# One recommendation tower, first stage: a DMA moved to another queue, one piece of work moved to ScalarE

## The reference

```python
e = stack([tbl_f[ids[:, f]] for f in range(27)], axis=1)      # 512 x 27 x 128
z = einsum('bnd,bmd->bnm', e, e)[:, i, j]                     # pairs i < j: 512 x 351
h = concatenate([z, dense_ctx], axis=1)                       # 512 x 367
h = maximum(h @ W_top1 + b_top1, 0)                           # 512
h = maximum(h @ W_top2 + b_top2, 0)                           # 256
y = h @ W_top3                                                # 512 x 1
```

## Time and profile before

| | us |
|---|---|
| median of 3 runs | 110.33 (110.22 to 110.46) |
| the profiled execution | 109.96 |
| its span in the profile | 107.8 |
| busy: PE, DVE, ACT, POOL | 99.6, 73.8, 70.4, 65.9 |

### The profile page before, as it was taken

One profiled execution on the slowest core, in us unless ns is written; L12 is line 12 of the kernel. 1 busy time (PEld: TensorE's weight loads), 2 busy tenths in 40 slices (PEclk: granted clock), 3 DMA queues, 4 the chain that ended last, 5 costly groups with the idle time before them and its releaser, 6 DMA issues.

```text
span 107.8 us, 2420 instructions
## 1 busy us (share of the span) xinstructions
PE 99.6 (92%) x993; PEld 84.2 (78%) x993; DVE 73.8 (68%) x68; ACT 70.4 (65%) x100; POOL 65.9 (61%) x71
## 2 busy tenths in 40 slices
PE   4995999999999799999999879999999999997992
PEld 4993887777767687876778679999998897996790
DVE  3299999999999999999999943035245405622131
ACT  5039999999999999999999956144404241421021
POOL 3177788777787777787777787777777720005000
PEclk9999999999999999999999999999999999999999
DMA  1899688888869694869526412679653443034100
GB/s 42 192 365 340 167 301 292 207 257 300 223 250 250 193 305 135 239 207 222 177 49 204 185 49 55 213 131 253 222 93 78 150 128 53 9 132 81 24 0 1
DMA packets 13031, 18.26 MB, mean 169 GB/s; under 512 B 7601, under 2 KB 8446, under 8 KB 13020
## 3 DMA queue, kind: packets, MB, share of 16 engines
q1 hardware_dynamic: 9552, 12.90, 39.8%
q0 software_dynamic: 2016, 4.06, 13.8%
q10 hardware_dynamic: 1452, 1.14, 3.5%
HBM read 16.32 MB, written 1.77 MB: 168 GB/s over the span
## 4 chain that ended last, share of the span: by engine, by line
PE 43%; DVE 37%; issue 9%; DMA 8%; ACT 1%; SPq 0%; ACTq 0%; DVEq 0%
DVE hot L474 25%; PE psG L359 13%; DVE parts L479 10%; PE psG L340 8%; PE psG L386 5%; PE psH L402 5%; PE psT L318 4%; DMA pick_ids<-in_picked_ids 4%; PE psH L340 3%; PE psH L371 3%; DMA pair_grams<-gram 3%; DMA zT<-pair_grams 2%; PE psH L417 1%; DVE hot L460 1%; DVE hot L463 1%
## 5 line engine op out<-in xcount | busy, mean ns | idle before, releaser
L301 POOL DMA_INDIRECT rows<-in_tbl,ids_sb x61 | 63.6, 1042 | 21.7 <-issue 18.3
L340 PE MATMUL psG<-hot,parts 128*128 128x512 f32 x196 | 49.5, 401 | 2.4 <-ACT hot L564 1.2
L340 PEld LDWEIGHTS psG<-hot,parts 128*128 128x128 f32 x196 | 35.2, 188 | 13.5 <-DVE hot L474 4.8
L474 DVE TENSOR_TENSOR hot<-pick_ids,psH 128x1536 fp32r<-128x1536 int32 (+2 forms) x23 | 41.5, 1843 | 0.0
L560 ACT ACTIVATE hot<-pick_ids,row_no 128x512 fp32r<-128x512 int32 (+1 forms) x30 | 19.4, 710 | 0.0
L479 DVE TENSOR_TENSOR parts<-table,parts 128x1024 fp32r<-128x1024 f32 (+1 forms) x12 | 16.2, 1349 | 0.0
L564 ACT ACTIVATE hot<-hot 128x1024 fp32r<-128x1024 f32 (+2 forms) x12 | 15.0, 1247 | 0.4
L359 PEld LDWEIGHTS psG<-ET 128*54 128x54 f32 x512 | 13.3, 130 | 2.3 <-issue 1.6
L359 PE MATMUL psG<-ET 128*54 128x54 f32 x512 | 13.9, 213 | 1.3 <-issue 1.2
L487 DVE COPY gram<-psG 128x432 f32<-128x432 f32 x8 | 7.3, 911 | 10.8 <-PE psG L359 10.8
L571 ACT COPY gram<-psG 128x432 f32<-128x432 f32 x8 | 7.3, 914 | 11.2 <-PE psG L359 10.5
(11 more groups left out here) (31 smaller groups left out, 49.7 us busy)
## 6 DMA issues: line engine op xcount, KB each, us to landing
table<-in_tbl SPq DMA_DIRECT2D x6, 640.0 KB, 4.8
table<-in_tbl SPq DMA_DIRECT2D x6, 512.0 KB, 5.5
pick_ids<-in_picked_ids SPq DMA_DIRECT2D x11, 256.0 KB, 4.0
rows<-in_tbl,ids_sb POOLq DMA_INDIRECT x61, 3.8
pair_grams<-gram SPq DMA_DIRECT2D x4, 216.0 KB, 2.3
pair_grams<-gram ACTq DMA_DIRECT2D x4, 216.0 KB, 3.0
w_sb<-in_w SPq DMA_DIRECT2D x1, 768.0 KB, 4.4
w_sb<-in_w SPq DMA_DIRECT2D x1, 512.0 KB, 4.3
```

Of the source, the lines that this page charges most:

```text
L301: pool.indirect_dma_start(out=rows[:, n % RING, x, :], out_offset=None, in_=gathered_tables[f], in_offset=bass.IndirectOffsetOnAxis(ap=ids ...
L340: last = pe.matmul(picked_psum(k), parts[:, k % 2, x, c, :], hot[:, k % 2, c, looked_up(k)], start=x == 0 and c == 0, stop=x == 1 and c == ...
L474: dve.tensor_tensor(hot[:, k % 2, first:end, looked_up(k)], pick_ids[:, k % TABLES, looked_up(k)].unsqueeze(1).to_broadcast(shape), number ...
```

## The change

The DMA of `ids_sb` goes from the head of SP's queue to ScalarE's queue, behind the one that ScalarE had. BY_ACT[0] becomes 3 instead of 2, so ScalarE makes three chunks of the first table's `hot` and VectorE five instead of six. Two of these three distances are computed ahead of `split_high(0)`, the third behind it.

```diff
-    BY_ACT = [2 if chunks == min(CH) else 3 for chunks in CH]
+    BY_ACT = [2 if chunks == min(CH) and k > 0 else 3 for k, chunks in enumerate(CH)]
...
         def _(sp):
-            sp.dma_start(ids_sb[:, :, :], ids).then_inc(ids_in, 16)
             for k in range(FP):
...
-            def make_last_hot(k):
-
+            def distances(k, chunks):
                 if k == 0:
                     act.wait_ge(first_ids_in, 16)
                 act.wait_ge(pick_ids_in[k], 16)
-                chunks = range(CH[k] - BY_ACT[k], CH[k])
                 for c in chunks:
                     act.activation(hot[:, k % 2, c, looked_up(k)], pick_ids[:, k % TABLES, looked_up(k)], ACT.Abs, bias=row_number(k, c),
                                    scale=-1.0).then_inc(distance_ready, 1)
+
+            def make_last_hot(k):
+                first = CH[k] - BY_ACT[k]
+                distances(k, range(first + 2 if k == 0 else first, CH[k]))
                 act.wait_ge(distance_ready, sum(BY_ACT[:k + 1]))
-                last = hot[:, k % 2, chunks[0]:CH[k], looked_up(k)]
+                last = hot[:, k % 2, first:CH[k], looked_up(k)]
                 act.activation(last, last, ACT.Relu, bias=1.0, scale=-1.0).then_inc(last_hot_ready, 1)
...
             act.dma_start(pick_ids[:, 0, 0:B // 2], picked_ids[0, 0:B // 2].partition_broadcast(V)).then_inc(first_ids_in, 16)
+            act.dma_start(ids_sb[:, :, :], ids).then_inc(ids_in, 16)
...
             act.wait_ge(row_no_ready, 2)
+            distances(0, range(CH[0] - BY_ACT[0], CH[0] - BY_ACT[0] + 2))
             split_high(0)
             make_last_hot(0)
```

## The result

The changed kernel takes 111.76 us as the median of four runs (111.27 to 112.93), the kernel before 110.28 in the same comparison (109.29 to 110.46): a ratio over the fast runs of 1.0186, with a 95% interval of 1.0131 to 1.0242. The two medians are 1.48 us apart, which is 1.3%, while the ratio says 1.9%: the change is slower, clear of noise, by 1.3 to 2.4%. I had forecast 110.6, within 109.7 to 111.1, so the measured time lies above the range. The profiled execution took 111.27 at a span of 109.4, against 109.96 at 107.8.

What follows compares the result with a forecast made beforehand. VectorE paced TensorE during the picks, ScalarE nearly level, GpSimd's gathers 0.85 us ahead of quad 15. TensorE's 0.55 gain is lost waiting for the delayed last gather: +0.23 on the 110.33 median gives 110.56, about 110.6 (109.7 to 111.1).

Steps and rivals of the forecast that it cites:

- hidden fourth chain: GpSimd's 61 gathers, absent from the chain of waits, run without gaps to quad 15, the last landing at 88.49.
- slack of 0.85 at quad 15: Before the change, the last gather lands at 88.49, only 0.85 us ahead of quad 15's weight loads at 89.34.
- the gain of the picks: At the handover from picks to first product, ScalarE's lead makes TensorE about 0.55 us earlier.
- the sign of being wrong: Last gather starting before 86.3 or after 88, or TensorE not stopping ahead of quad 15, would refute the prediction.
- The hold and the lost place: Gathers starting inside line 479's subtraction are held to its end; the third, not fourth, is held, losing one place.
- the landing of `ids_sb`: At the kernel's start, `ids_sb` lands between 4.6 and 5.6, taken as 5.0, 0.85 us later than now.
- rival C: At the first subtraction, the second gather is held, two places lost: another 1.25 us, 111.8; chance 0.16.
- VectorE's gain: At the first table, line 479 starts at 7.83 instead of 8.19, 0.36 us earlier, set by the table's landing.
- From the split to the next table's: ScalarE's work behind the first table's landing takes 3.15 us instead of 3.37, saving 0.22.
- transfers that hang on it: From handover to quad 15, TensorE's work and dependent transfers carry the 0.55 us gain through, reaching quad 15 at 88.8.

Runs made afterwards that it cites:

- e7: Changed kernel with line 478's second operand read from PSUM (low parts not the reference's): 109.44 us against 109.42 for the kernel before, ratio 1.0010.
- e9: Kernel before plus a GpSimd memset of 2500 columns between the landing of `ids_sb` and the first gather: 110.32 us against 109.35, ratio 1.0110.
- e10: Kernel before plus a GpSimd memset of 3200 columns between the landing of `ids_sb` and the first gather: 111.4 us against 109.35, ratio 1.0154.
- e11: Kernel before with `ids_sb` second on ScalarE's queue and the small b1 load in its place at SP's head: 110.06 us, ratio 1.0062.
- e1: Changed kernel with `ids_sb` back at the head of SP's queue: 149.9 us against 150.4 in a slow batch, times not used.
- e5: Changed kernel with `ids_sb` back at the head of SP's queue, on another chip: 109.48 us against 109.42 for the kernel before, ratio 1.0001.
- e8: Kernel before plus a GpSimd memset of 500 columns between the landing of `ids_sb` and the first gather: +0.4 us, ratio 1.0028.
- e2: Kernel before with only the DMA of `ids_sb` moved to ScalarE's queue: 153.0 us against 150.4 in a slow batch, times not used.
- e4: Changed kernel with `ids_sb` issued by GpSimd: 153.3 us against 150.4 for the kernel before in a slow batch, times not used.
- e6: Kernel before with only the DMA of `ids_sb` moved to ScalarE's queue, on another chip: 112.16 us against 109.42, ratio 1.0288.
- e3: Changed kernel with ScalarE's two queued DMAs exchanged, `ids_sb` first: 151.3 us against 150.4 for the kernel before in a slow batch, times not used.
- e12: Changed kernel with `ids_sb` at SP's head and the first table second on ScalarE's queue: 110.5 us, ratio 1.0122 to the kernel before.

## Why the prediction was wrong

*The bound and the hidden fourth chain: right.* The gathers' slack of 0.85 at quad 15 was the thing to watch; the gain of the picks (ScalarE's copy at 61.46, forecast 61.4; first product at 62.16, forecast 62.05) came to nothing, and TensorE stopped where I said, for 1.66 us instead of 0.7. The last gather started at 88.29, behind the 88 that I gave as the sign of being wrong.

*The hold and the lost place: right, and shown by e7, e9 and e10.* The Trainium skill, "SBUF — State Buffer", section "SBUF: two separate sides", lists two kinds of VectorE operation that take the pair of ports from GpSimd: one in a two-port mode, which I cited, and one with two SBUF inputs, the latter only against a GpSimd operation that reads SBUF. e7 points to the second: with one operand from PSUM the duration stays at 1.22 and every hold is gone. So does the kernel before: a gather that starts inside the comparison of line 474, which has one operand in SBUF and one in PSUM, isn't held (6.58 for 0.98, in the 1.75 us from 6.51 on).

*The step that failed: the landing of `ids_sb`, "1.17 + 3.4 = 4.6 at the earliest and 1.17 + 4.4 = 5.6 at the latest", of which I took 5.0.* It landed at 6.6. The upper bound was the wrong row: the 4.4 us of the second DMA on SP's queue was measured with nothing of SP's moved forward, and e11 gives 4.6 us for that case, 0.2 beside it. I had priced SP's earlier transfers as a gain for the table, and not as a load on what was issued with them; that is 0.8 us. With `ids_sb` 2.45 late instead of 0.85 the second gather, not the third, met the subtraction. So rival C was the case, to which I gave 0.16, and the range left it out. That its price, 111.8, is the measured 111.76 is partly luck: C's last gather would start at 86.88 + 1.25 = 88.13, and it started at 88.29; and four runs between 111.27 and 112.93 don't fix a median to 0.05.

*VectorE's gain: half of what I took.* 0.18 instead of 0.36. I moved the table's landing and not that of the first ids, which took 4.3 us instead of 3.9 and were used at 5.14 instead of 4.71: the same omission. On this the runs agree: the first ids took 3.5 to 3.9 in the seven traces with SP's transfers at their old times (before, e1, e5, e8, e9, e10, e11), and 4.2 to 4.7 in the five with them early (after, e2, e4, e6, e7). The table didn't hold VectorE up: its split began at 6.48, forecast 6.66, and the high part was there before the comparison had ended.

*ScalarE: right in size.* From the split to the next table's 9.66 - 6.48 = 3.18 us, forecast 3.15. What I missed is that its lead can be given back at the transfer of block 1, where I had written "transfers that hang on it"; so it was in the profiled executions of the changed kernel and of e5, and not in that of e7. Why stays open: SP saw the writes landed 3.8 to 3.9 us after their issue in all three, against 3.2 before, and its six loads took 3.2 to 3.9 to issue, 4.1 before; no run takes either apart.

*The other way.* e5 says that without the queue part the change makes no difference that can be measured.

## What to carry to other kernels

A stream without gaps beside the critical path has to be followed to its last consumer before anything that feeds its start is delayed; here 2.45 us at the start, 80 us ahead of the consumer, were the whole result. Where two engines fall into step once per period, as here, a delay isn't passed on as it is but in whole places: ask which instruction comes next when the other engine takes the lock. A slack read from one execution is that execution's; here it differed by 0.6 us between executions. And when DMAs are reordered at the start of a kernel, all that are issued within the same microsecond or two are to be priced again, each against the new company.

## What the runs showed of the hardware

- A gather that starts inside a subtraction ends 0.80 to 0.85 us behind the subtraction's end, in every kernel but e7, with the one exception of e11 below. One already under way isn't held: it passed even when it began only 0.07 us ahead of the subtraction (e9). In e11 gather 2 began at 8.23, 0.02 behind the start of the subtraction at 8.21, and took 0.98, while the subtraction took 1.28 instead of 1.22: there it seems that VectorE waited, for 0.06 us.
- Between the landing of `ids_sb` and the first gather lie 0.85 to 1.0 us in all kernels without a memset there (4.14 to 5.11 before, 6.6 to 7.56 after); in e8 a memset of 0.51 fits into them, and in e9 and e10 the first gather starts 0.18 behind the memset.
- The 32 KB of `ids_sb`, issued second on ScalarE's queue, took 5.3 to 5.7 us with SP's transfers early (after, e2, e6, e7), and 4.6 with them at their old times (e11). They took 4.3 at the head of ScalarE's queue (e3) and 5.6 alone on GpSimd's (e4), both with SP's transfers early, and 3.1 to 3.4 at the head of SP's queue (before, e1, e5, e8, e9, e10, e12).
